# Start of a four-stage transformer kernel: identity products, load order, an early Exp, and the first norms in smaller groups

## The reference, cut to what matters

```python
def _layernorm(x, axis=-1, eps=1e-05):
    m = jnp.mean(x, axis=axis, keepdims=True)
    v = jnp.var(x, axis=axis, keepdims=True)
    return (x - m) / jnp.sqrt(v + eps)
...
x = x + _L0_xattn_ref(_layernorm(x, axis=-1), ctx_1024, ctx_1024, ...)   # 16 heads of 16
x = x + _L0_ffn_ref(_layernorm(x, axis=-1), ...)                         # 8 experts, 112 rows each
x = x + _L1_xattn_ref(_layernorm(x, axis=-1), ctx_1024, ctx_1024, ...)
x = x + _L1_ffn_ref(_layernorm(x, axis=-1), ...)
```

## Time and profile before

| | us |
|---|---|
| median of 3 runs | 386.39 |
| lowest, highest | 385.32, 388.12 |
| the profiled execution, its own time | 388.26 |
| its span, first to last instruction | 386.5 |

### The profile page before, as it was taken

One profiled execution on the slowest core, in us unless ns is written; L12 is line 12 of the kernel. 1 busy time (PEld: TensorE's weight loads), 2 busy tenths in 40 slices (PEclk: granted clock), 3 DMA queues, 4 the chain that ended last, 5 costly groups with the idle time before them and its releaser, 6 DMA issues.

```text
span 386.5 us, 7920 instructions
## 1 busy us (share of the span) xinstructions
PE 363.0 (94%) x3108; PEld 273.4 (71%) x3108; DVE 184.6 (48%) x565; ACT 147.9 (38%) x357; POOL 57.1 (15%) x95
## 2 busy tenths in 40 slices
PE   3889999999999999999899999999389999999997
PEld 2546665766567566656688898998368879888875
DVE  4864445556664574654262112111469756622500
ACT  0424553644445535434443221120024657513210
POOL 2720000010101010100020000030774420200000
PEclk9999999999999999998999999999669999999999
DMA  8936060605201000000207399960210011021000
GB/s 243 351 89 220 0 220 2 218 15 168 64 3 33 9 14 1 3 13 3 66 14 208 118 301 336 329 189 24 60 36 2 3 51 51 10 66 48 25 23 25
DMA packets 24853, 35.29 MB, mean 91 GB/s; under 512 B 2560, under 2 KB 21376, under 8 KB 24704
## 3 DMA queue, kind: packets, MB, share of 16 engines
q1 hardware_dynamic: 22128, 31.73, 25.8%
q0 software_dynamic: 768, 1.84, 1.6%
q10 hardware_dynamic: 1920, 1.21, 1.1%
HBM read 31.06 MB, written 3.72 MB: 90 GB/s over the span
## 4 chain that ended last, share of the span: by engine, by line
PE 52%; issue 2%; ACT 2%; DVE 1%; ACTq 0%; DVEq 0%
PE ps L572 7%; PE ps L715 7%; PE ps L582 7%; PE ps L693 6%; PE ps L474 5%; PE ps L647 3%; PE ps L663 2%; PE ps L637 2%; PE ps L349 1%; PE ps L451 1%; PE ps L428 1%; PE ps L706 1%; ACT heads L827 1%; PE ps L723 1%; PE ps L679 1%
## 5 line engine op out<-in xcount | busy, mean ns | idle before, releaser
L1045 DVE TENSOR_REDUCE mneg<-ps 112x2 f32<-112x750 f32 x64 | 57.1, 934 | 42.6 <-PE ps L414 42.3
L827 ACT ACTIVATE heads<-ps 125x896 f32<-125x896 f32 x48 | 41.4, 915 | 20.5 <-PE ps L434 20.5
L1259 POOL TENSOR_TENSOR rstd<-veps,neghalf 112x1 f32<-112x1 f32 x32 | 18.3, 573 | 200.5 <-DVE veps L1011 200.3
L414 PE MATMUL ps<-heads 32*112 32x375 f32 x256 | 38.8, 518 | 1.6 <-DVE mneg L1045 1.0
L358 PE MATMUL ps<-ctxT,w_in 128*128 128x375 f32 x64 | 27.0, 547 | 7.4 <-DMA ctxT<-in_ctxT 6.0
L428 PE MATMUL ps<-heads 32*125 32x224 f32 x384 | 33.0, 374 | 0.7 <-DVE mneg L1045 0.3
L572 PEld LDWEIGHTS ps<-xT,ring 128*128 128x128 f32 x256 | 29.8, 192 | 1.2 <-ACT xT L782 0.7
L572 PE MATMUL ps<-xT,ring 128*128 128x112 f32 x256 | 29.9, 275 | 0.5 <-ACT xT L782 0.5
L715 PE MATMUL ps<-heads,ring 128*112 128x256 f32 x128 | 28.8, 382 | 0.0
L582 PE MATMUL ps<-ring,heads 128*112 128x256 f32 x128 | 28.8, 379 | 0.0
L451 PEld LDWEIGHTS ps<-heads,vones 125*17 125x17 f32 x768 | 17.5, 98 | 14.7 <-issue 12.1
(11 more groups left out here) (139 smaller groups left out, 533.1 us busy)
## 6 DMA issues: line engine op xcount, KB each, us to landing
ring<-in_L_ffn_W SPq DMA_DIRECT2D x16, 1024.0 KB, 6.6
ctxT<-in_ctxT SPq DMA_DIRECT2D x8, 375.0 KB, 11.3
heads<-in_L_ffn_W SPq DMA_DIRECT2D x2, 1024.0 KB, 9.6
ring<-x_by_odd_rows_dram SPq DMA_DIRECT2D x4, 448.0 KB, 3.6
ring<-in_mask SPq DMA_DIRECT2D x1, 1312.5 KB, 7.2
expert_in_dram<-eo SPq DMA_DIRECT2D x1, 896.0 KB, 11.0
b2row<-in_L_ffn_b SPq DMA_DIRECT2D x8, 112.0 KB, 7.7
out_dram<-ring SPq DMA_DIRECT2D x8, 112.0 KB, 2.0
```

The costliest lines, as they stand in the source:

```text
L414: mm = pe.matmul(bank(j)[0:S, 0:S2], qz[rows, m, a, b * S:(b + 1) * S], kt[b % 3][rows, m, :], start=True, stop=True)
L827: act.activation(pT[w % 2][0:KC, pair.start:pair.stop, :], ps[0:KC, pair.start:pair.stop, 0:2 * QW], ACT.Exp, scale=DK ** -0.5).then_inc(f ...
L1045: v.tensor_reduce(mneg[:, b % 2, PAIRS * g + pair.start:PAIRS * g + pair.stop], ps[0:S, pair.start:pair.stop, 0:S2], AX.X, ALU.max, negate ...
```

## The change

Five parts. (1) PE runs `WARM` = 10 products of the identity with itself into bank 5, right after the identity is ready and before it waits for Wk; nothing reads them. (2) ACT issues the bias columns first. (3) After the third DMA issue ACT waits for the identity and takes an Exp of one number, which nothing reads, so that its function table is asked for there; the other six loads are issued behind it. (4) DVE norms only batches 0 and 1 before the steps; batches 2 and 3 follow at the end of slot (-1, 6), 4 and 5 at the end of slot (0, 5), 6 and 7 at the end of slot (2, 6); the second-norm counters are reckoned in the new order. (5) POOL's roots and its additions of the bias row follow in the same slots, and stage C3 waits for the addition of its own batch and not for all eight.

```diff
--- before.py
+++ after.py
@@ -47,9 +47,12 @@
     6: [("U", 0), ("C5", 1), ("K1", -2), ("ND1", -1)],
 }
 FIRST_K = 1
+WARM = 10
 
 QW, QCHUNKS, FIRST_Q = 2 * S, NB // 2, 1
 Q_SLOTS = {2: "QX", 3: "QP"}
+
+FIRST_NORMS = {(-1, 6): (2, 3), (0, 5): (4, 5), (2, 6): (6, 7)}
 
 
 
@@ -113,8 +116,14 @@
 def norm_orders():
 
 
-    moments = [(n, b) for n in (1, 2) for b in range(NB)] + [(3, 0)]
-    rows = [(n, b) for n in (1, 2) for b in range(NB)]
+    moments = [(1, 0), (1, 1)]
+    rows = [(1, 0), (1, 1)]
+    for i, u in steps():
+        moments += [(2, b) for stage, b in extras(i, u) if stage == "C3"]
+        rows += [(2, b) for stage, b in extras(i, u) if stage == "L2"]
+        moments += [(1, b) for b in FIRST_NORMS.get((i, u), ())]
+        rows += [(1, b) for b in FIRST_NORMS.get((i, u), ())]
+    moments += [(3, 0)]
     for i in range(AT_STEPS):
         moments += [(3, b) for b in combined_in(i)]
         rows += [(4, i - 5)] * (0 <= i - 5 < NB - 1)
@@ -199,6 +208,7 @@
         blocks = sb("blocks", [P, P // DK])
         parity = sb("parity", [P, 2])
         bq_par = sb("bq_par", [P, DT, 2])
+        unread = sb("unread", [1, 1])
         rden = sb("rden", [S, H])
         tri = sb("tri", [S, S], BF16)
         onesb = sb("onesb", [S, S], BF16)
@@ -360,7 +370,7 @@
                     mm.then_inc(filled[n], 1)
 
             def turn_x(c):
-                pe.wait_ge(xn_ready, 2 * (c + 1))
+                pe.wait_ge(xn_ready, ROWS_DONE[1, 2 * c + 1])
                 for b in (2 * c, 2 * c + 1):
                     transpose_x("XT1", b, next_bank(SPARE))
 
@@ -393,6 +403,9 @@
 
 
             pe.wait_ge(consts, 1)
+
+            for _ in range(WARM):
+                pe.matmul(bank(5)[:, 0:P], ident[:, :], ident[:, :], start=True, stop=True)
             pe.wait_ge(ld["wk"], 16)
             project_k(0, [0])
             turn_x(0)
@@ -518,7 +531,7 @@
                         mm = pe.matmul(o[0:S, 0:D], ccT[:, k, :], w_in[:, 3, k, :], start=k == 0, stop=k == DT - 1)
                     mm.then_inc(filled[n], 1)
                 elif stage == "C4":
-                    pe.wait_ge(xn_ready, NB + b + 1)
+                    pe.wait_ge(xn_ready, ROWS_DONE[2, b])
                     transpose_x("XT2", b, next_bank(SPARE))
                 elif stage == "C5":
                     read(("XT2", b))
@@ -767,9 +780,11 @@
                 return None if n in (LOW, HIGH) else bank(n), drained[n]
 
 
+            act.dma_start(bcol[:, :, :], A["bias_columns"]).then_inc(ld["bias"], 16)
             act.dma_start(w_in[:, 1, :, :], A["L0_xattn_Wk"].rearrange("(k p) n -> p k n", p=P)).then_inc(ld["wk"], 16)
             act.dma_start(w_in[:, 0, :, :], A["L0_xattn_Wq"].rearrange("(k p) n -> p k n", p=P)).then_inc(ld["wq"], 16)
-            act.dma_start(bcol[:, :, :], A["bias_columns"]).then_inc(ld["bias"], 16)
+            act.wait_ge(consts, 1)
+            act.activation(unread[:, :], ident[0:1, 0:1], ACT.Exp)
             act.dma_start(w_in[:, 2, :, :], A["L0_xattn_Wv"].rearrange("(k p) n -> p k n", p=P)).then_inc(ld["wv"], 16)
             act.dma_start(w_in[:, 3, :, :], A["L0_xattn_Wo"].rearrange("(k p) n -> p k n", p=P)).then_inc(ld["wo"], 16)
             act.dma_start(wg[:, :, :], A["L0_ffn_Wg"].rearrange("(k p) n -> p k n", p=P)).then_inc(ld["wg"], 16)
@@ -1023,20 +1038,22 @@
             v.memset(seen[:, :, :], 0.0).then_inc(ones_ready, 1)
             v.memset(onesc[:, :], 1.0).then_inc(ones_ready, 1)
             v.memset(mpieces[:, :, :, :], 0.0).then_inc(ones_ready, 1)
-            for n, group in enumerate((range(0, 2), range(2, NB))):
-                v.wait_ge(ld_x[n], 16)
+            def first_norms(group):
                 for b in group:
                     moments(b)
                 for b in group:
                     normalise(1, b)
-                if n == 0:
-                    v.wait_ge(parity_ready, 1)
-                    step(v.tensor_reduce(parity[:, :], blocks[:, :].rearrange("p (j a) -> p a j", a=2), AX.X, ALU.add))
-                    v.wait_ge(ld["bias"], 16)
-                    v.tensor_tensor(bq_par[:, :, :], bcol[:, 0, :].unsqueeze(2).broadcast_to([P, DT, 2]),
-                                    parity[:, :].unsqueeze(1).broadcast_to([P, DT, 2]), ALU.mult)\
-                     .then_inc(bq_par_ready, 1)
+
+            v.wait_ge(ld_x[0], 16)
+            first_norms((0, 1))
+            v.wait_ge(parity_ready, 1)
+            step(v.tensor_reduce(parity[:, :], blocks[:, :].rearrange("p (j a) -> p a j", a=2), AX.X, ALU.add))
+            v.wait_ge(ld["bias"], 16)
+            v.tensor_tensor(bq_par[:, :, :], bcol[:, 0, :].unsqueeze(2).broadcast_to([P, DT, 2]),
+                            parity[:, :].unsqueeze(1).broadcast_to([P, DT, 2]), ALU.mult)\
+             .then_inc(bq_par_ready, 1)
             v.wait_ge(ones_ready, 8)
+            v.wait_ge(ld_x[1], 16)
 
 
             def row_max(b, g):
@@ -1069,7 +1086,7 @@
                      .then_inc(free, 1)
                 elif stage == "C3":
                     o, free = full(("C3", b))
-                    v.wait_ge(xbo_ready, NB)
+                    v.wait_ge(xbo_ready, b + 1)
                     v.tensor_tensor(xres[:, b, :], o[0:S, 0:D], xres[:, b, :], ALU.add).then_inc(free, 1)
                     drained_by_me(("C3", b))
                     moments(b)
@@ -1120,6 +1137,7 @@
                 for stage, b in extras(i, u):
                     if stage in ("ND0", "ND1", "C1", "C3", "L2", "C5", "D5", "C6", "D6"):
                         post(stage, b)
+                first_norms(FIRST_NORMS.get((i, u), ()))
 
 
             v.wait_ge(ld["b1"], 16)
@@ -1273,7 +1291,7 @@
             g.affine_select(out=blocks[:, :], in_=blocks[:, :], compare_op=ALU.is_ge, fill=0.0, base=DK - 1,
                             pattern=[[DK, P // DK]], channel_multiplier=-1).then_inc(parity_ready, 1)
             g.wait_ge(ones_ready, 1)
-            for b in range(NB):
+            for b in range(2):
                 root(1, b)
 
             step(g.memset(onesb[:, :], 1.0))
@@ -1287,11 +1305,13 @@
             g.iota(spill[:, :], pattern=[[S, NB]], base=T, channel_multiplier=1,
                    allow_small_or_imprecise_dtypes=True).then_inc(consts, 1)
 
-            g.wait_ge(xn_ready, NB)
+            def add_bo(b):
+                g.wait_ge(xn_ready, ROWS_DONE[1, b])
+                g.tensor_tensor(xres[:, b, :], xres[:, b, :], browL0[:, :], ALU.add).then_inc(xbo_ready, 1)
+
             g.wait_ge(ld["rows"], 16)
-            for b in range(NB):
-                g.tensor_tensor(xres[:, b, :], xres[:, b, :], browL0[:, :], ALU.add).then_inc(xbo_ready, 1)
-            g.wait_ge(xbo_ready, NB)
+            for b in range(2):
+                add_bo(b)
 
             for i, u in steps():
                 for stage, b in extras(i, u):
@@ -1303,6 +1323,11 @@
                         g.wait_ge(slots_ready, b + 1)
                         g.indirect_dma_start(out=xg_dram, out_offset=bass.IndirectOffsetOnAxis(
                             ap=idx_put[:, b:b + 1], axis=0), in_=xn[:, b, :], in_offset=None).then_inc(put, 16)
+                for b in FIRST_NORMS.get((i, u), ()):
+                    root(1, b)
+                for b in FIRST_NORMS.get((i, u), ()):
+                    add_bo(b)
+            g.wait_ge(xbo_ready, NB)
 
 
 
```

## The result

The changed kernel takes 395.8 us (median; 392.8 to 397.7) beside 386.4 us for the kernel before: a ratio of 1.023, 95% interval 1.019 to 1.027. Measured again beside other kernels it gave 1.016 (1.010 to 1.022). The forecast was 387.9 us with a range from 384.3 to 390.8; the measured time lies 5 us above its upper end, and even the fastest of the four executions (392.8) is outside. The profiled execution took 397.72 us with a span of 395.9.

A forecast was written before the change was run, and what follows sets the result against it. PE, busy 94% of the span, was taken as the bound. The front's -1.4 us plus norm stalls of 1.77 and 1.16 gave +1.5 us on 386.39, so 387.9 us, range 384.3 to 390.8.

The forecast's parts named there:

- Identity products, table load, PE's new front: Before the steps: ten products 2.0 to 6.3, Exp 1.30 us out of chain, PE's chain ends 11.5 to 12.6.
- The wait for `wg` is what is late next: At the start of the steps: `wg` lands at 13.7 and PE, ready earlier, waits until 13.8.
- Gain: 15.23 - 13.8 = 1.4 us: Front: PE enters the first step at 13.8 instead of 15.23, 1.4 us gained; ends 0.1 and 3.7.
- The late issue costs nothing: ACT's load queue: loads issued up to 1.3 us later behind the early Exp cost nothing; Wv has over 3 us.
- Norms in slot (-1, 6): Step -1: the 2.57 us pair fits in DVE's 3.13 us idle time and costs nothing.
- Norms in slots (0, 5) and (2, 6): In the steps: the norm pairs delay DVE's reductions and so PE's scores, costing 1.77 and 1.16 us.
- rival 3: PE's idle gaps make the clock fall again; 3.5 us at half speed costs about 1.7 us: 389.6; chance 0.14.
- The signs of being wrong: Wrong if first step before 12.5, batch 1 hole under 1 us, or first reduction to batch 0 scores changes length.
- rival 1: Front: `wg` lands early enough that PE never waits, all of 3.7 us gained: 385.6; chance 0.18.
- rival 2: Steps: the norm stalls are half absorbed by shrinking waits in later slots: 386.5; chance 0.12.
- the whole front with no stall: Faster than 382.5 us needs the whole front and no stall at all; chance 0.04.
- rival 4: Front: identity products don't raise the clock before 13.7, front gives 0.1, steps cost 2.93: 389.2; chance 0.09.

The follow-up runs named there:

- the mended kernel: Changed kernel with norms moved to slots (0, 4) and (2, 4) and output and gate weight waits moved to their readers: 385.8 us, 0.995 of the kernel before.
- front_only: Kernel before plus ten identity products, bias columns first and early Exp, all norms staying in the front: 390.8 us, ratio 1.006.
- gg_bias_third: The mended kernel with the bias columns third on ACT's queue, behind Wk and Wq: 386.3 us, 0.997 of the kernel before.

## Why the prediction was wrong

- *Identity products, table load, PE's new front*: right. 20 rows in 4.1 us from 1.93, clock full at 5.3 (forecast 6.3 to 9.7, so earlier than its best), queries issued at 9.88. One wait was missed: Wk and Wq land at 6.1 and 9.7, since the bias columns ahead cost Wq 3 us and not 0.5.
- *The wait for `wg` is what is late next*: right in kind, mis-sized. It landed at 14.5 instead of 13.7, so the step "Gain: 15.23 - 13.8 = 1.4 us" measured 0.55 us. "The late issue costs nothing" holds for the table load (Wv was issued at 2.35, while it ran), but not for the whole queue: `wg` was issued 0.2 us later and took 0.6 us longer.
- *Norms in slot (-1, 6)*: right, no shift of its own.
- *Norms in slots (0, 5) and (2, 6)*: right in place and mechanism; 2.2 and 1.8 us against 1.77 and 1.16. The terms were mis-sized because the pair's 2.57 us was taken from a stretch in which POOL added nothing, and the new place puts its addition beside the second norm.
- *The clock*: this is the step that failed. The sum, -1.4 + 1.77 + 1.16, has no term for it; the forecast has it as rival 3, "The clock falls again", with a chance of 0.14 and one fall of 1.7 us. There were four new ones, 5.2 us in this execution, and a longer stretch at half clock near 290 us, 1.4 more. Without the four the changed kernel would lie at 390.6 (an estimate, the median less this execution's falls), just inside the range; the rest of the miss is the 0.9 us of the front and the 1.1 us of the stalls. Each hole was treated as if it cost its own length only, though the text had found three of the four holes at whose places the falls then came; the fourth, 0.98 us in step -1, is in both kernels. The trace of before had shown that a fall needs no long idle time: the clock fell at 174.2 us with PE busy for 2.76 us of the 3.2 us ahead of it. I read only the long wait at 272 us and so took falls for rare. The size of one fall, 3.5 us at half speed, was about right (3.4), but does not follow from the stretch of 4.7 us that the text names for it; the fall at 174.2 would have given it.
- *The signs of being wrong*: the first two did not come (first step at 14.68, hole at batch 1 of 1.65 us), the third did. From the first reduction to the scores of batch 0 it was 10.1 us before (17.19 to 27.29) and is 11.7 (17.56 to 29.30): the fall at 25.7.
- *Small slips in its sums*: four rows in 2.63 us are 0.66 each and not 0.63; rivals 1 and 2 together give 384.2, not 384.3; and the whole front with no stall gives 382.7, which is not below 382.5. None of them bears on the miss.
- *Rivals 1, 2, 4*: no. The front gave 0.55 and not 3.7, nothing of the stalls was absorbed (the shift stays within 0.02 us from 59 to 100 us), and the clock did rise early.

The signs of the parts were therefore right, and what the chances had wrong is their independence: in this execution every stall in the steps came with a second cost behind it, and over all profiles every second one did.

## What to carry to other kernels

On an engine that sets the time, price a new hole at its own length plus, in about half of the cases here, a stretch at half clock behind it that costs 0.9 to 1.7 us, and look for the slot in which the other engine is idle before moving work into the steps: a shift by one and two slots was worth about 1% here. An engine that is woken early only pays if no wait follows; take the next gate away first (the waits for weights that nobody reads yet), since warming alone gave 1.001 and without it the mended kernel was as fast.

## What the runs showed of the hardware

- The clock fell behind holes of 1.0 to 3.1 us, with PE busy 92% of the stretch from 29.3 to 53 us, at five of ten places with a new hole and at none of eighteen without. The changed kernel's two profiled executions differ in number and place of the falls (five short ones and four), and a kernel's time follows its mean granted clock (2.6 us per 0.01 in front_only; 2.5 to 5.3 over the six kernels with ten executions).
- The granted clock of the profile reads 1.00 in the kernel before from the start, yet the rows up to 13.6 us run at half the later rate; only the distance between starts shows it.
- Five KB of bias columns at the head of ACT's queue landed in 2.8 us and made a 256 KB load two places behind land some 3 us later (9.7 us in the changed kernel, against 6.6 in gg_bias_third).
- ACT's queue goes on issuing DMAs while a table load runs (issue at 2.35, load 2.29 to 3.57).
- What stays open: why a hole is followed by a fall in one execution and not in the next, and what makes the half-clock stretch near 290 us 13.7 us long in ten profiles and 17.1 in four. Neither was tried.
